# A graph layer on one core: the W_self product moved behind the loop, the sum of keys moved to VectorE, the mix laid out anew

## What is computed

```python
xn = _layernorm(x)
# graph layer
h_s, z = xn @ W_self.T, xn @ W_func.T
e = leaky_relu(concat(z[src], z[dst], w) @ W_att.T)
agg = segment_sum(softmax_by_dst(e)[:, None] * z[src], dst)
gnn = xn + relu(where(deg > 0, h_s + agg, xn))
# mix
q_phi, k_phi = phi(xn @ Wq + bq), phi(xn @ Wk + bk)      # phi(a) = a + 1 if a > 0 else exp(a)
kv, k_sum = k_phi.T @ (xn @ Wv + bv), k_phi.sum(nodes)    # by head
out = (q_phi @ kv) / (q_phi @ k_sum + 1e-6) @ Wo + bo
y = _layernorm(xn + out); mix = _layernorm(y + relu(y @ W1 + b1) @ W2 + b2)
x = x + gnn + mix
x = x + experts(_layernorm(x))
```

## Time and profile before

| | |
|---|---|
| median of three runs (range) | 2118.76 us (2105.8 to 2121.87) |
| the profiled execution, its span | 2118.82 us, 2117.1 us |
| TensorE (matmul) busy | 1836.2 us, 87% |
| VectorE busy | 1342.8 us, 63% |
| ACT busy | 1127.6 us, 53% |
| POOL busy | 1342.4 us, 63% |
| mean granted TensorE clock | 0.923 of 2.4 GHz |

### The profile page before, as it was taken

How to read it: one execution, slowest core, us unless ns; L and a number is a source line. 1 busy time by engine, 2 the same in 40 slices (tenths; PEclk the granted TensorE clock), 3 DMA queues, 4 the chain that set the end, 5 groups by cost and what they waited for, 6 DMA issues and landing times.

```text
span 2117.1 us, 37394 instructions
## 1 busy us (share of the span) xinstructions
PE 1836.2 (87%) x9585; PEld 1386.4 (65%) x9585; DVE 1342.8 (63%) x3843; ACT 1127.6 (53%) x3416; POOL 1342.4 (63%) x1095
## 2 busy tenths in 40 slices
PE   6799987998988889989888988899977789999991
PEld 5555555766666667666666666677644479899980
DVE  6653456676667767766676677666665756455574
ACT  4445545665555556655565555565643345555550
POOL 4075658787777778877777777778400525754376
PEclk9889988999999999999999999889998889999995
DMA  7888945666666666666666666555449535555464
GB/s 211 249 189 180 219 117 146 173 182 166 163 165 162 161 159 166 172 163 170 166 173 165 164 165 162 147 144 150 109 109 232 165 97 148 167 161 147 137 184 118
DMA packets 329757, 345.16 MB, mean 163 GB/s; under 512 B 138731, under 2 KB 278393, under 8 KB 329548
## 3 DMA queue, kind: packets, MB, share of 16 engines
q1 hardware_dynamic: 187212, 198.98, 33.9%
q0 software_dynamic: 135360, 137.34, 27.8%
q10 hardware_dynamic: 6975, 6.45, 1.0%
HBM read 255.18 MB, written 86.27 MB: 161 GB/s over the span
## 4 chain that ended last, share of the span: by engine, by line
PE 64%; DVE 13%; issue 7%; ACT 7%; SPq 3%; DMA 3%; DVEq 2%; POOL 1%; ACTq 0%; POOLq 0%
PE bank L758 61%; DVE acc L1868 3%; SPq L438 2%; POOL g_all L745 1%; DVEq L1868 1%; DVE work L1726 1%; ACT spare L1222 1%; PE bank L1091 1%; DMA g_all<-sorted_d 1%; ACT work L1256 1%; DVE attr_s L1518 1%; ACT work L1236 1%; PE bank L922 1%; ACT work L1235 1%; ACT work L1227 1%
## 5 line engine op out<-in xcount | busy, mean ns | idle before, releaser
L718 POOL DMA_INDIRECT wexp<-func_rows,a_src x850 | 1062.3, 1250 | 411.1 <-issue 186.6
L1868 DVE SCALAR_TENSOR_TENSOR acc<-acc,corr,bank 125x257 f32 x850 | 404.2, 476 | 440.0 <-PE bank L758 383.0
L758 PE MATMUL bank<-wexp,onehot 125*125 125x257 f32 x1700 | 546.9, 434 | 30.1 <-DVE acc L1868 26.1
L1265 ACT ACTIVATE onehot<-iota_r,a_rel 125x125 f32<-125x125 f32 x850 | 332.2, 391 | 332.0 <-PE bank L758 329.2
L758 PEld LDWEIGHTS bank<-wexp,onehot 125*125 125x125 f32 x1700 | 313.0, 204 | 117.0 <-ACT onehot L1273 40.2
L1273 ACT ACTIVATE onehot<-onehot,a_p 125x125 f32<-125x125 f32 x850 | 328.4, 386 | 0.0
L735 POOL DMA_INDIRECT sorted_d<-acc,work x100 | 122.6, 1226 | 224.5 <-DVE acc L1977 143.7
L758 PE MATMUL bank<-g_all,wexp 128*128 128x128 f32 x1840 | 227.1, 277 | 3.1 <-ACT g_all L1386 2.0
L758 PE MATMUL bank<-work,w_s 128*128 128x250 f32 x800 | 204.9, 377 | 23.7 <-ACT work L1256 23.6
L758 PEld LDWEIGHTS bank<-g_all,wexp 128*128 128x128 f32 x1840 | 216.5, 193 | 5.0 <-ACT g_all L1386 2.4
L745 POOL DMA_INDIRECT g_all<-y_d,work x100 | 131.2, 1312 | 116.5 <-DVE g_all L2147 65.3
(11 more groups left out here) (282 smaller groups left out, 2587.1 us busy)
## 6 DMA issues: line engine op xcount, KB each, us to landing
rel_oh<-rel_d SPq DMA_DIRECT2D x50, 531.2 KB, 6.0
attr_s<-in_attr SPq DMA_DIRECT2D x100, 224.0 KB
sorted_d<-spare SPq DMA_DIRECT2D x72, 256.0 KB
work<-in_x SPq DMA_DIRECT2D x75, 224.0 KB
g_all<-sorted_d SPq DMA_DIRECT2D x115, 128.0 KB
y_d<-g_all SPq DMA_DIRECT2D x115, 128.0 KB
wexp<-func_rows,a_src POOLq DMA_INDIRECT x850
work<-xnT_d SPq DMA_DIRECT2D x50, 250.0 KB, 5.7
```

Of the source, the lines that this page charges most:

```text
L718: pool.indirect_dma_start(ring[:, n % RING, :], None, func_rows, bass.IndirectOffsetOnAxis(ap=a_src[:, n // CS, n % CS:n % CS + 1], axis=0 ...
L758: return pe.matmul(o, l, r, start=first, stop=last_, **kw)
L1265: act.activation(onehot[:, n % AHEAD, :], iota_r[:], ACT.Abs, bias=a_rel_v[:, n:n + 1], scale=-1.0).then_inc(s("far"), 1)
L1868: v.scalar_tensor_tensor(to, to, corr[:, k % 2, y:y + 1], bank[stepping[n % 3]][0:R, 0:D + 1], ALU.mult, ALU.add).then_inc(s("summed"), 1)
```

## The change

- **The W_self product** leaves the loop. Its four matmuls, ACT's copy, the store and the tensor `self_rows` go. Behind the loop SP loads `xnT_d` of the group in place of the W_self rows (one DMA for two), TensorE makes the four matmuls there in place of the two with the identity, `have_self` goes, and VectorE's `rows` has four instructions where two were: sum times 1/denominator plus xn, then the product times "has edges" plus that.
- **The sum of keys**: two matmuls less per group in `kv_sum`; VectorE adds phi of each group to `phi_all` (`kv_count`), and behind the last group two matmuls with ones sum it over the partitions.
- **The mix**: most pieces are cut in two and stand in other slots; `xn_in` and `m_y` get two buffers each; x is loaded at 2 instead of 8.

```diff
+HIDDEN_AT = (25, 26, 27, 28, 29, 32, 33, 34)
+DOWN_AT = (37, 38, 39, 40, 43, 44, 45, 46)
...
             def kv_sum(g):
...
                     for c in range(2):
-                        mm(bank[6][:, c * D:(c + 1) * D], k_x[g % KB][:, j, c * 128:(c + 1) * 128], p_phi[g % PB][:, j, :],
+                        last = mm(bank[6][:, c * D:(c + 1) * D], k_x[g % KB][:, j, c * 128:(c + 1) * 128], p_phi[g % PB][:, j, :],
                            False, g == GROUPS - 1 and j == 1, skip_group_check=True)
-                    last = mm(bank[5][0:1, 0:D], ones_c[0:R, :], p_phi[g % PB][:, j, :],
-                              False, g == GROUPS - 1 and j == 1, skip_group_check=True)
                 last.then_inc(s("kv_sum"), 1)
+                if g == GROUPS - 1:
+                    pe.wait_ge(s("phi_sum"), GROUPS + 1)
+                    mm(bank[5][0:1, 0:D], ones_c[0:R, :], phi_all[:, 0, :], True, False)
+                    mm(bank[5][0:1, 0:D], ones_c[0:R, :], phi_all[:, 1, :], False, True).then_inc(s("kv_done"), 1)
...
                 for g, at in mix_at(n):
...
-                    if at == 1:
...
-                        queries(g)
-                    if at == 10:
+                    if at in (0, 1):
+                        queries(g, at)
+                    if at == 5:
                         attention(g)
-                    if at == 8:
-                        self_part(g)
-                    if at == 18:
-                        project(g)
-                    if at == 27:
+                    if at in (11, 12):
+                        project(g, at - 11)
+                    if at == 23:
                         turn(g)
-                    if 0 <= at - PERIOD - 3 < FC:
-                        hidden(g, at - PERIOD - 3)
...
+                    if at in HIDDEN_AT:
+                        hidden(g, HIDDEN_AT.index(at))
+                    if at in DOWN_AT:
+                        down(g, DOWN_AT.index(at) // 4, DOWN_AT.index(at) % 4)
...
-            def residual(g):
+            def self_part(g):
...
-                mm(to, ident[0:R, 0:R], c_xn[k], True, False)
-                pe.wait_ge(s("c_have"), 2 * g + 2)
-                mm(to, ident[0:R, 0:R], c_self[k], False, True).then_inc(s("c_gnn"), 1)
+                for j in range(2):
+                    for c in range(2):
+                        last = mm(pr_(2 + 2 * (g % 2))[:, j, :], c_xnT[k][:, c, j * R:(j + 1) * R], wself_s[:, c, :], c == 0, c == 1)
+                last.then_inc(s("c_gnn"), 1)
...
+            def kv_count(g):
+                v.wait_ge(s("phi"), 2 * (g + 1))
+                v.wait_ge(s("phi_sum"), g + 1)
+                v.tensor_tensor(phi_all, phi_all, p_phi[g % PB], ALU.add).then_inc(s("phi_sum"), 1)
...
                 for g in kv_at(n - 1):
                     kv_phi(g)
+                    kv_count(g)
...
             def rows(g):
...
                 for j in range(2):
-                    v.scalar_tensor_tensor(c_x1[k][:, j], accv[:, 2 * g + j, 1:D + 1], rden[:, 2 * g + j:2 * g + j + 1],
-                                           pr_(2 + 2 * k)[:, j], ALU.mult, ALU.add).then_inc(s("c_r"), 1)
+                    b = 2 * g + j
+                    o.did(v.scalar_tensor_tensor(c_x1[k][:, j], accv[:, b, 1:D + 1], rden[:, b:b + 1], c_xn[g % CBUF][:, j],
+                                                 ALU.mult, ALU.add))
+                v.wait_ge(s("c_gnn"), g + 1)
+                o.settle()
+                for j in range(2):
+                    b = 2 * g + j
+                    v.scalar_tensor_tensor(c_x1[k][:, j], pr_(2 + 2 * k)[:, j], have[:, b:b + 1], c_x1[k][:, j], ALU.mult,
+                                           ALU.add).then_inc(s("c_r"), 1)
```

More of the change, by code:

```diff
@@ L617, in group_in @@
                 freed(sp, s("c_x1"), g - CBUF + 1)
-                for to, rows in ((c_self, self_rows), (c_xn, xn_rows), (c_x2, mix_rows)):
+                load(f"group_in{g % CBUF}", c_xnT[g % CBUF].rearrange("p c n -> p (c n)"), xnT_d[g])
+                for to, rows in ((c_xn, xn_rows), (c_x2, mix_rows)):
                     load_rows(f"group_in{g % CBUF}", to[g % CBUF], rows_of(rows, g))
@@ L1291, in select @@
                     shares(n + STOCK)
-            def self_copy(i):
-                act.wait_ge(s("l_self_ps"), i + 1)
-                freed(act, s("self_out"), 32 * i)
-                act.activation(l_self, pr_(0), ACT.Copy).then_inc(s("l_self"), 1)
             act.wait_ge(s("affine"), 2)
```

238 lines of the change are left out of this document (110 added, 128 removed).

## The result

The changed kernel takes 2056.62 us in the median of four runs (2049.44 to 2058.03), the kernel before 2112.97 in the four runs beside them (2105.8 to 2121.87): a ratio of 0.9725, 95% interval 0.9673 to 0.9776. The profiled execution took 2049.44 us with a span of 2047.6, 69.4 us less than the profiled one of before. Predicted were 2058, with a range of 2030 to 2096.

The account below looks back on a forecast made before the run. TensorE was taken to bound the loop by 2.1 us per period, with POOL's gathers the next limit; 2118.8 - 21 (keys) - 42 (loop) - 6 (tail) + 8 (behind the loop) = 2058 us, range 2030 to 2096.

Parts of the forecast that it names:

- The loop: In the loop of steps, TensorE's period falls to POOL's gather pace of 46.4 us per 30 steps: -42 us.
- the 3 us kept back: Held off the loop's capped gain of 45.3 us, for runs in which PE still holds a gather.
- certain: In the loop, 1.72 us of PE per period from the removed W_self product, of 2.1 needed to reach POOL's pace.
- Gathers that get quicker too: Rival, chance 0.09: in the loop the 0.03 us above the median gather vanish, 23 us more, 2035 us.
- The mix anew: In the loop, new slots change TensorE's waits and shorten its plain stretch: -3.4 to +1.7 us per period.
- The sum of keys: Up to step 50, ones_c matmuls leave TensorE: 13 us before step 0, 9 after, +1 at the end, -21 together.
- The other way out that I priced, 17 us: For the keys' sums on DVE: if the cover failed, 25 x 0.68 = 17 us.
- The port: Rival, chance 0.06: DVE's key sums hold POOL's gathers, 10 us before step 0 and 7 after, some hidden: 12 us, 2070.
- Behind the loop: In the stage putting rows together, VectorE's extra pair adds 0.9 us to 12 second-half groups, less small savings: +8 us.
- The tail: From last gather to last step, 56 us before, 47 plus 3 for the gather after: -6 us.
- the slower rival: Rival, chance 0.08: in the loop hidden runs at half clock behind the plain stretch, net +3.0 us a period, 2178 us.

Follow-up runs that it names:

- three sums: The changed kernel with every sum of the keys made three times on VectorE (50 more sums of 125x512): 2086.95 us in one run.
- the keys alone: The kernel before with only the sum of the keys moved to VectorE, W_self and the mix as before: 2097.49 us, ratio 0.9914 to before.

## Why the prediction was right, and which sizes were off

Between the two profiles 69.5 us of span went. By the first table: 4.5 ahead of the first gather (scatter), 15.1 from there to step 50, 46.8 from step 50 to the last gather, 6.2 in the tail, and 0.9 and 2.2 more behind the loop and in the experts. The prediction had -21, -42, -6 and +8.

- **The loop (-42; measured -46.8).** Right, and for the reason given: TensorE was 2.1 us per period above the gathers' pace, and the pace caps the gain. Half of `down` left out moves the period by 0.02 us, shorter gathers move it by 2.8. True waits of the gathers behind step 50 went from 47.0 us to 0.9 (45.3 to 0.6 between gathers 150 and 800), which is 46.1 of the 46.8, so the 3 us kept back weren't needed. That 1.72 us of the product alone are "certain" was too much: it brought 1.4, though the gathers' pace already held that kernel in places (`of_source` waited 19.9 us in eight runs). Gathers that get quicker too, the rival of that name, didn't come: the mean is 1.243 us where it was 1.244.
- **The mix anew.** Nothing speaks against the bounds of -3.4 to +1.7 per period. The old waits at relu and turn shrank as expected, and new tightness cost 18.5 us at the attention; at the gathers' pace neither shows in the time. What the layout is worth beyond 0.66 us per period can't be seen behind that pace.
- **The sum of keys (-21; measured -15.1).** The mechanism holds, the size doesn't. The step that failed is "with DVE under half busy I cost it at nothing". It shows in the 50 steps: ahead of step 0 13 us were put down and 14.3 came, behind it 9 were put down and 0.8 came. A busy share of half doesn't say what stands ahead of the instruction that TensorE waits for. No sums at all bring 5 us, and the same sums behind the step's part 6.7. The other way out that I priced, 17 us, was too much.
- **The port** (third rival). The mechanism is in the trace, the size isn't. In the changed kernel 15 gathers begin inside a sum. The 13 with 0.18 us or more of it left end 1.08 or 1.09 us after the sum's end and take 1.27 to 1.71 us; gathers that begin ahead of a sum take their usual 1.21. VectorE and POOL in order of time, the longest of them and the next:

```profile
255.21 0.69 DVE L1517 TENSOR_TENSOR work<-work 125x512 f32<-125x512 f32 x1
255.28 1.71 POOL L717 DMA_INDIRECT wexp<-func_rows,a_src  x1 [0.30 <-issue]
...
257.29 1.21 POOL L717 DMA_INDIRECT wexp<-func_rows,a_src  x1 [0.30 <-issue]
```

  The Trainium skill's rule (SBUF — State Buffer, section "SBUF: two separate sides") would have a sum hold a gather, and the trace agrees. But a gather waits only for what is left of the sum, and 12 of the 25 sums hold none: 3.1 us in all, 1.9 of it behind step 0, where the rival had 17 with 5 hidden. A median over gathers "beside a sum" hides it (1.215 against 1.214 us with three sums), since most of those began ahead of it. In the loop the same is seen without any sum: 92 of the 688 gathers from 384 to 1448 us take over 1.26 us, 20.0 us above the median together. All 22 that began inside L1498, a product of two tensors in SBUF, with 0.18 us or more of it left, are among them; of 142 that began so inside the step's part L1853, one of whose inputs is a bank, 1 is.
- **Behind the loop (+8; measured +0.9).** Groups follow at 5.03 us, 1.00 more than before, where 0.86 was put down for the pair; it takes 0.99 with the time to the next instruction, and the new wait for ACT takes the place of one for TensorE. It holds in both halves. The gain against it is in the first twelve groups, 67.6 us before and 60.4 now. But that code took 61.8 us in the kernel with the keys alone, where it is the same as before: the loads' waits scatter, and against that profile the stage is 6.5 us longer.
- **The tail (-6; measured -6.2)**, and the slower rival: it came in part. In 14 of the 25 groups hidden's first eight instructions follow the plain stretch at full speed, four in 1.01 us as at 793.19; in the other 11 one to seven of them run slower, as at 749.41, where the granted clock is at the lower level, 0.50 from 749.4 to 750.7. Over the loop 63 of hidden's 800 instructions take over 0.5 us, before 4 of 768, and 6 of the queries' 192 where it was 58. So the low clock moved from the queries to hidden and wasn't saved, but it reaches 63/4/25 = 0.6 slots a group, and that rival decides from 2.7. The 1.7 us that it had for the queries was the reading of one group: 58 of 192 make 58/24 x 0.21 = 0.5 a period. The loop's mean clock is 0.94, before 0.92.

```profile
749.41 1.87 PE L757 MATMUL bank<-work,w_s 128*128 128x250 f32 x4
...
790.77 1.04 PE L915 MATMUL bank<-ident,work 125*128 125x125 f32 x4
...
793.19 1.01 PE L757 MATMUL bank<-work,w_s 128*128 128x250 f32 x4
```

- **The sum.** That 2058 lies 1.4 us from the median is in part luck. Keys brought 6 us less than forecast and the stage behind the loop cost 7 less, which cancel. The forecast also started from 2118.8, where the median of before is 2112.97: by medians the gain is 56.4 us where 61 were forecast, and the two profiles, of which the changed one is the shortest of its runs, have 69.5. The sizes by stage are those of this one pair.

## What to carry to other kernels

Before pricing an edit on the busiest engine, add up the floor of each engine that is tied to it (here the mean gather plus the spacing that remains when nothing is late): the distance to the nearest floor is all that the edit can bring, and a wait list by line shows afterwards whether it was reached. An instruction put on a half-idle engine is free only if nothing that the bound engine waits for stands behind it in that engine's order, so place it behind, not ahead. Look at how single instructions of another engine lie beside it, not at a median over many. And where an engine waits once per group for a factor that another engine makes, put work that needs only loads between the two.

## What was not expected of the hardware

A gather's cost here goes by its rows: 1.214 us for 125 and 1.011 for 100, by these two sizes some 8 ns a row and 0.2 us beside them (an estimate), with 0.30 us more before the next. A gather that begins while VectorE works on two tensors in SBUF stands still until that instruction ends: it ends 1.08 or 1.09 us behind it, beside the sums up to 1.71 us after its start. And waits of TensorE can cost twice: with three sums 14.2 us more of waits came with 15.4 us more of busy time for the same products, at a mean clock of 0.86 instead of 0.93.
